# Attention scores of two layers: contraction groups of 32 rows with two masked key copies in four half-filled PSUM banks, in place of groups of 64 rows with four copies in two full banks

## The chip, the cores and the metric

The kernel runs on one core of one Trainium2 chip. The metric is the device time of one execution in microseconds (us), as the median of several executions. Lower is better. All arithmetic is fp32.

## The reference, cut to what matters

32 sequences of 64 tokens and 256 features go through four layers. Layer 0 is a small cross attention, layers 1 and 2 are transformer blocks (self attention, cross attention with a context, MLP), and layer 3 is a recurrent block. The change is in layers 1 and 2:

```python
NH = 16; HD = 16                      # 16 heads of 16 features
def attention(q, k, v, mask):
    scores = jnp.einsum('bhqd,bhkd->bhqk', q, k) / jnp.sqrt(jnp.float32(HD))
    scores = scores * mask - 10000.0 * (1.0 - mask)
    probs = jax.nn.softmax(scores, axis=-1)
    return jnp.einsum('bhqk,bhkd->bhqd', probs, v)
...
qkv = layernorm(hidden_states, ln1_s, ln1_b) @ w_qkv + b_qkv
q, k, v = jnp.split(qkv, 3, axis=-1)
ctx = merge_heads(attention(split_heads(q), split_heads(k), split_heads(v), ltor_mask))
x = hidden_states + ctx @ w_ao + b_ao
q = layernorm(x, ln2_s, ln2_b) @ w_q + b_q
k, v = jnp.split(encoder_states @ w_kv + b_kv, 2, axis=-1)
ctx = merge_heads(attention(split_heads(q), split_heads(k), split_heads(v), cross_mask))
x = x + ctx @ w_co + b_co
return x + gelu(layernorm(x, ln3_s, ln3_b) @ w1 + b1) @ w2 + b2
```

## The kernel before

`phase_a` is layer 0, `phase_b` is layers 1 and 2, and `phase_c` is layer 3. In `phase_b` the 2048 tokens are four groups of 512 tokens, and two layers make eight **turns** (`TURNS`), each for one group in one layer. A turn has eight **steps** k: 0 to 3 are self attention and 4 to 7 cross attention, each for 128 tokens (two sequences of 64). Turns 1 to 6 are one hardware loop. All engines follow an order written out by hand in their function `turn`, and they meet only through semaphores.

Heads have 16 features and a matmul operand starts at row 0, 32, 64 or 96, so heads are not multiplied one by one. The keys are written several times, each copy with all heads but one of every group of rows set to zero (`keys` on ACT, which multiplies by the 0/1 column `lane[:, m]` and adds a bias that is zero elsewhere; `NM` copies). One matmul then gives the scores of `NM` heads of one group of rows. Before the change a group is 64 rows (`HALF`), with `NM` = 4.

PSUM has eight banks of 512 fp32 columns. `SC, PT, CX, CO, YB = 0, 2, 4, 5, 6`: the scores (`SC`) take banks 0 and 1, the transposed probabilities (`PT`) banks 2 and 3, and the projections and the MLP banks 6 and 7.

One step of attention passes over four engines:

- `scores(n, k)` on PE: before the change eight matmuls of 64 rows, 64 stationary and 256 moving columns. Each fp32 matmul is two passes, and each pass is one record in the trace. They wait until DVE has read the scores of tile k-1 (`mul_ok`).
- `mask(n, k)` on DVE (L1346): reads the scores out of PSUM, multiplies by the mask and raises `mul_ok`. `add_mask` on POOL (L786) adds the other half of the mask.
- `maximum` (L1353) and `subtract` (L1358) on DVE, `exps` on ACT (L1204).
- `probs_T(n, k)` on PE (L983): eight transposes into banks 2 and 3, after `exp_ok`. `copy_pT` on ACT (L1209) copies them out.
- `times_v` on PE (L998) waits for that copy; then DVE `normalize` (L1364, L1366), PE `result_T` (L1006) and ACT `copy_cT` (L1214).

PE issues `scores(k+2)` right behind `times_v(k)`, so the scores of tile k+1 are written before `probs_T(k)` and those of tile k+2 after it. Steps 3 and 4 of `turn` on PE read:

```python
times_v(n, 3)
next_scores(n, 3, nxt)      # scores of tile 5
hidden(prev, 5, nxt)        # L1036, MLP of the turn before
probs_T(n, 4)
result_T(n, 3)
norm_T_mid(n, 2)            # L899
norm_T_in(nxt, prev)        # L893
queries_mid(n, 2)           # L956
```

DVE does in step 3: `maximum` of tile 4, `pre` 3, `subtract` of tile 4, `residual` 2, `pre` 4, `normalize` 3, `norm` 2, `pre` 5 (L1404), and then `mask` of tile 5. The self-attention keys of the first group are made at the end of `phase_a`, chunk 0 on ACT (L472) and chunk 1 on DVE (L553).

Of the kernel before, what the change touches and what calls it, by code (L numbers as in the profile page):

```python
# [17 lines left out]
ALU = mybir.AluOpType  # L18
# [3 lines left out]
P = 128  # L22
B, S, D = 32, 64, 256
# [5 lines left out]
NC = D // P  # L29
NH, HD = 16, 16  # L30
NPAIR = NH // 2
HALF = P // 2
NM = HALF // HD
VW = HD + 1
DFF = 1024
NJ = DFF // P
# [12 lines left out]
def packed(**sets):  # L49

    cols, spans, at = {}, {}, 0
    for s, parts in sets.items():
        start = at
        for n, width in parts:
# [8 lines left out]
                              out=(("co", D),), hidden=(("w1", DFF),))  # L63
VL, VL_SETS, VL_COLS = packed(first=(("ln1_s", 2), ("ln1_b", 2), ("bq", 2), ("bk", NC * NM)),
                              middle=(("ln2_s", 2), ("ln2_b", 2), ("bq2", 2), ("bk2", NC * NM)),
                              hidden=(("ln3_s", 2), ("ln3_b", 2), ("b1", NJ)))
# [507 lines left out]
def phase_b(nc, io, ps, w, x_mid, ld_b, ld_c, ld_set, zero_ok, a_stored, b_loads, entry, stored, c_loads, head):  # L574

    ctx = ExitStack()
    with ctx:
# [3 lines left out]
        def sem(name):  # L581
            return ctx.enter_context(nc.semaphore("b_" + name))
# [13 lines left out]
        qT, kB, vP = ([w[a + n] for a in ("self", "cross")] for n in ("_q", "_k", "_v"))  # L596
        sc = w["sc"]
# [19 lines left out]
        sc_ps, mul_ok, add_ok, max_ok, sub_ok, exp_ok = (sem(n) for n in ("sc_ps", "mul_ok", "add_ok", "max_ok", "sub_ok", "exp_ok"))  # L617
# [8 lines left out]
        TILES = 2 * NP  # L626
# [11 lines left out]
        def tile(n, k):  # L638

            return TILES * n + k  # L640
# [6 lines left out]
        SC, PT, CX, CO, YB = 0, 2, 4, 5, 6  # L647
# [212 lines left out]
        def _(pe):  # L860
# [99 lines left out]
            def scores(n, k):  # L960
                a, p = k // NP, k % NP
                if a == 1:
                    pe.wait_ge(q_ok[1], tile(n, 2 * p) + 2)
                if p == 0:
                    pe.wait_ge(k_ok[a], 2 * n + 2)
                    if a == 0:
                        pe.wait_ge(q_ok[0], 2 * n + 2)
                after(pe, mul_ok, tile(n, k))
                pe.sem_inc(sc_go, 1)
                for c in range(NC):  # L970
                    for half in range(2):
                        f = slice(half * HALF, (half + 1) * HALF)
                        for b in range(2):
                            t = (2 * p + b) * S
                            mm = pe.matmul(ps[b * S:(b + 1) * S, SC + half, c * D:(c + 1) * D], qT[a][f, c, t:t + S],
                                           kB[a][f, c, 2 * p + b, :, :].rearrange("f m k -> f (m k)"), start=True, stop=True)
                mm.then_inc(sc_ps, 1)

            def probs_T(n, k):
                pe.wait_ge(exp_ok, tile(n, k) + 1)  # L980
                for half in range(2):
                    for i in range(NPAIR // 2):
                        mm = pe.transpose(ps[:, PT + half, i * P:(i + 1) * P],  # L983
                                          sc[:, k % 2, half, 2 * i:2 * i + 2, :].rearrange("q i k -> q (i k)"), w["ident"][:, :])
                    mm.then_inc(pT_ps, 1)
# [79 lines left out]

            def turn(n, prev, nxt):

                probs_T(n, 0)
                last_project(n, 0, prev)
                keys_ctx(n, 0, prev)  # L1070
                times_v(n, 0)
                next_scores(n, 0, nxt)
                keys_ctx(n, 1, prev)
                result_T(n, 0)
                values_ctx(n, 0)

                probs_T(n, 1)
                last_project(n, 1, prev)
                values_ctx(n, 1)
                times_v(n, 1)  # L1080
                next_scores(n, 1, nxt)
                norm_T_mlp(prev, n)
                result_T(n, 1)
                norm_T_mid(n, 0)
                hidden(prev, 0, nxt)
                queries_mid(n, 0)

                probs_T(n, 2)
                last_project(n, 2, prev)
                hidden(prev, 1, nxt)  # L1090
                times_v(n, 2)
                next_scores(n, 2, nxt)
                hidden(prev, 2, nxt)
                hidden(prev, 3, nxt)
                result_T(n, 2)
                norm_T_mid(n, 1)

                probs_T(n, 3)
                queries_mid(n, 1)
                hidden(prev, 4, nxt)  # L1100
                last_project(n, 3, prev)
                times_v(n, 3)
                next_scores(n, 3, nxt)
                hidden(prev, 5, nxt)
                probs_T(n, 4)
                result_T(n, 3)
                norm_T_mid(n, 2)
                norm_T_in(nxt, prev)

                queries_mid(n, 2)  # L1110
                queries_in(nxt, 0)
                last_project(n, 4, prev)
                times_v(n, 4)
                next_scores(n, 4, nxt)
                queries_in(nxt, 1)
                result_T(n, 4)
                norm_T_mid(n, 3)
                keys_in(nxt, 0)
                queries_mid(n, 3)

                probs_T(n, 5)
                last_project(n, 5, prev)
                keys_in(nxt, 1)
                times_v(n, 5)
                next_scores(n, 5, nxt)
                hidden(prev, 6, nxt)
                result_T(n, 5)
                hidden(prev, 7, nxt)

                probs_T(n, 6)  # L1130
                last_project(n, 6, prev)
                values_in(nxt, 0, prev)
                times_v(n, 6)
                next_scores(n, 6, nxt)
                mlp_out(prev, 0, nxt)
                result_T(n, 6)
                mlp_out(prev, 1, nxt)

                probs_T(n, 7)
                last_project(n, 7, prev)  # L1140
                values_in(nxt, 1, prev)
                times_v(n, 7)
                next_scores(n, 7, nxt)
                mlp_out(prev, 2, nxt)
                result_T(n, 7)
                mlp_out(prev, 3, nxt)
# [8 lines left out]
            n = TURNS - 1  # L1155
# [134 lines left out]
        def _(dve):  # L1290
# [49 lines left out]
            def mask(n, k):  # L1340
                a, p = k // NP, k % NP
                if a == 1 and p == 0:
                    dve.wait_ge(cmask_ok, 2 * n + 2)
                dve.wait_ge(sc_ps, tile(n, k) + 1)
                m = (self_mul[:, :], cross_mul[:, p, :])[a]
                dve.tensor_tensor(sc[:, p % 2, :, :, :].rearrange("q f i k -> q (f i) k"),  # L1346
                                  ps[:, SC:SC + 2, :].rearrange("q f (i k) -> q (f i) k", k=S),
                                  m.unsqueeze(1).broadcast_to([P, NH, S]), ALU.mult).then_inc(mul_ok, 1)

            def maximum(n, k):  # L1350
                dve.wait_ge(add_ok, tile(n, k) + 1)
# [171 lines left out]
            n = TURNS - 1  # L1523
# [1276 lines left out]
```

## Time and profile before

| | |
|---|---|
| median of 3 runs | 1195.87 us (1191.57 to 1198.06) |
| span of the profiled execution | 1193.7 us |
| busy share of the span | PE 90%, PE weight loads 60%, DVE 70%, ACT 46%, POOL 36% |
| records of matmul passes | 8032 |
| matmul passes of the scores (L975) | 1024, 71.8 us busy |
| key copies on ACT (L1197) | 120 activations, 83.8 us |
| length of a turn in the loop, from one `probs_T(n, 0)` to the next | 89.4 us |

The span goes from the first to the last instruction of one profiled execution; the page gives no other time of that execution, and the runs without the profiler are a separate measurement. The busy digits of an engine are tenths of one fortieth of the span. PEclk is the clock that was granted to TensorE, in tenths of full speed. In a timeline row the first number is the start, the second the length of the merged piece, and the bracket gives how long the engine sat idle before it and what released it. A piece of several matmuls holds as many passes as its x count says.

### The profile page before, as it was taken

To read this page: it belongs to the slowest core of one execution; us is meant where nothing else is said; L and a number is where in the kernel's file an instruction comes from. 1 tells how busy PE (TensorE), PEld (TensorE's weight loads), DVE (VectorE), ACT (ScalarE), POOL (GpSimd) and SP (SyncE) were. 2 spreads that over 40 slices of the span, in tenths; PEclk is the share of its full clock that TensorE was granted. 3 is DMA by queue.
4 is the path that set the end of the run, shared out by engine and by line. 5 is a ranking of instruction groups with operands and counts; after the bars stand their busy time and mean duration, and the time that the engine had idled before them with its cause. 6 is when DMAs were issued, how large, how long until landed. Compare 5 with 4: busy or idle time off the path is not lost. (4 is left out here: it accounts for less than half of the span.)

```text
span 1193.7 us, 21696 instructions
## 1 busy us (share of the span) xinstructions
PE 1070.6 (90%) x8032; PEld 714.9 (60%) x8032; DVE 832.5 (70%) x1575; ACT 546.1 (46%) x1016; POOL 433.2 (36%) x387
## 2 busy tenths in 40 slices
PE   7987797999999999999999999978986888979866
PEld 6875565668668668668668668656363353443524
DVE  3665776876876876876876876873448687796864
ACT  4653453474474474474474474462231434414331
POOL 2111443442442442442442442331317427264250
PEclk9998978999999999999999999999997999989998
DMA  7130100001002002102101001030010010010100
GB/s 251 62 98 18 42 1 19 24 2 36 22 0 71 22 0 79 35 0 67 60 0 35 22 1 35 1 122 18 1 36 21 1 36 20 0 35 3 36 1 18
DMA packets 37952, 40.28 MB, mean 34 GB/s; under 512 B 8640, under 2 KB 33536, under 8 KB 37648
## 3 DMA queue, kind: packets, MB, share of 16 engines
q1 hardware_dynamic: 37776, 39.55, 10.3%
q8 instruction: 29, 0.48, 0.2%
q14 instruction: 19, 0.16, 0.0%
q0 software_dynamic: 128, 0.10, 0.0%
HBM read 31.26 MB, written 8.39 MB: 33 GB/s over the span
## 5 line engine op out<-in xcount | busy, mean ns | idle before, releaser
L1353 DVE TENSOR_REDUCE b_neg_max<-head_area 128x16 f32<-128x1024 f32 x64 | 77.8, 1216 | 89.2 <-POOL head_area L786 88.7
L791 POOL TENSOR_TENSOR b_rstd<-b_var,minus_half 128x1 f32<-128x1 f32 x63 | 34.5, 548 | 250.0 <-DVE b_var L1382 250.0
L2101 POOL TENSOR_TENSOR c_rs<-c_st,head_area 128x512 f32<-128x512 f32 x64 | 88.7, 1415 | 97.3 <-DVE c_st L2580 95.7
L1204 ACT ACTIVATE head_area<-head_area 128x1024 f32<-128x1024 f32 x64 | 68.0, 1062 | 112.1 <-DVE head_area L1358 111.6
L1036 PE MATMUL ps<-b_hT_mlp,wl 128*128 128x512 f32 x224 | 108.9, 608 | 7.5 <-DVE b_act_g L1404 6.3
L1050 PE MATMUL ps<-w,b_act_g 128*128 128x256 f32 x448 | 102.8, 383 | 2.7 <-ACT b_act_g L1222 2.7
L786 POOL TENSOR_TENSOR head_area<-head_area,b_self_add 128x1024 f32<-128x1024 f32 x32 | 75.4, 2355 | 79.5 <-DVE head_area L1346 79.5
L786 POOL TENSOR_TENSOR head_area<-head_area 128x1024 f32<-128x1024 f32 x32 | 75.3, 2354 | 77.1 <-DVE head_area L1346 77.1
L1209 ACT ACTIVATE head_area<-ps 128x512 f32<-128x512 f32 x128 | 70.1, 607 | 63.0 <-PE ps L983 62.9
L1050 PEld LDWEIGHTS ps<-w,b_act_g 128*128 128x128 f32 x448 | 82.9, 190 | 17.6 <-issue 4.6
L869 PE MATMUL ps<-head_area,wl 128*128 128x512 f32 x176 | 85.9, 611 | 0.0
L1358 DVE TENSOR_TENSOR head_area<-head_area,b_neg_max 128x1024 f32<-128x1024 f32 x64 | 78.1, 1220 | 1.2
L2580 DVE TENSOR_TENSOR_SCAN c_st<-head_area,ps 128x512 f32<-128x512 f32 x64 | 73.7, 1203 | 3.8 <-ACT ps L2388 3.8
L983 PE MATMUL ps<-ident,head_area 128*128 128x128 f32 x512 | 70.1, 282 | 4.2 <-ACT head_area L1204 4.2
L1019 PE MATMUL ps<-wl,b_cT 128*128 128x256 f32 x252 | 68.3, 395 | 2.9 <-ACT b_cT L1214 1.4
L983 PEld LDWEIGHTS ps<-ident,head_area 128*128 128x128 f32 x512 | 61.2, 146 | 15.4 <-issue 8.1
L1036 PEld LDWEIGHTS ps<-b_hT_mlp,wl 128*128 128x128 f32 x224 | 38.6, 190 | 49.9 <-issue 30.5
L879 PE MATMUL ps<-wl,head_area 128*64 128x128 f32 x1024 | 64.5, 280 | 0.2 <-ACT head_area L1197 0.2
L879 PEld LDWEIGHTS ps<-wl,head_area 128*64 128x64 f32 x1024 | 57.0, 140 | 9.7 <-issue 7.2
L1214 ACT ACTIVATE b_cT<-ps 128x256 f32<-128x256 f32 x64 | 24.6, 384 | 77.2 <-PE ps L1006 77.2
L1019 PEld LDWEIGHTS ps<-wl,b_cT 128*128 128x128 f32 x252 | 45.0, 194 | 15.2 <-issue 6.9
L1396 DVE TENSOR_TENSOR b_x_out<-ps,b_x_mlp 128x256 f32<-128x256 f32 x28 | 11.9, 425 | 57.0 <-PE ps L1050 48.6
(262 smaller groups left out, 2321.1 us busy)
## 6 DMA issues: line engine op xcount, KB each, us to landing
head_area<-x_mid SPq DMA_DIRECT2D x9, 512.0 KB, 3.8
wl<-in_wl SPq DMA_DIRECT2D x4, 1024.0 KB, 6.9
head_area<-in_ctxT SPq DMA_DIRECT2D x8, 512.0 KB, 3.6
x_mid<-b_x_out SPq DMA_DIRECT2D x8, 512.0 KB, 2.9
area<-in_wc SPq DMA_DIRECT2D x1, 2336.0 KB, 8.1
a_x_in<-in_x SPq DMA_DIRECT2D x16, 128.0 KB, 3.0
a_y_in<-in_ctx SPq DMA_DIRECT2D x16, 128.0 KB, 3.7
w<-in_w SPq DMA_DIRECT2D x2, 1024.0 KB, 9.5
```

Of the source, the lines that this page charges most:

```text
L786: pool.tensor_tensor(t, t, m.unsqueeze(1).broadcast_to([P, NH, S]), ALU.add).then_inc(add_ok, 1)
L869: mm = pe.matmul(ps[:, YB + c, :], weight(name, k, first + c * P, first + (c + 1) * P), rhs[:, k, :], start=(k == 0), stop=(k == NC - 1))
L879: mm = pe.matmul(ps[odd * S:(odd + 1) * S, YB + half, b * P:(b + 1) * P], lhs[:, k, t:t + S], weight(name, k, odd * P, (odd + 1) * P), sta ...
L983: mm = pe.transpose(ps[:, PT + half, i * P:(i + 1) * P], sc[:, k % 2, half, 2 * i:2 * i + 2, :].rearrange("q i k -> q (i k)"), w["ident"][ ...
L1019: mm = pe.matmul(ps[:, CO, OUT], cT[:, half, p * P:(p + 1) * P], weight(("ao", "co")[a], half), start=(half == 0), stop=(half == 1))
L1036: mm = pe.matmul(ps[:, YB + j % 2, :], weight("w1", k, j * P, (j + 1) * P), hT_mlp[:, k, :], start=(k == 0), stop=(k == NC - 1))
L1050: mm = pe.matmul(ps[:, YB + MLP_BANK[p], 0:D], act_g[:, j, p * P:(p + 1) * P], w["w2"][:, j, :], start=(j == 0), stop=(j == NJ - 1))
L1209: act.activation(pT[:, b, :, :].rearrange("k i q -> k (i q)"), ps[:, PT + b, :], ACT.Copy).then_inc(pT_ok, 1)
L1353: dve.tensor_reduce(neg_max[:, k % 2, :], t, AX, ALU.max, negate=True).then_inc(max_ok, 1)
L1358: dve.tensor_tensor(t, t, neg_max[:, k % 2, :].unsqueeze(2).broadcast_to([P, 2 * NPAIR, S]), ALU.add).then_inc(sub_ok, 1)
L2101: pool.tensor_tensor(rs[:, i % BUFS, :], st[:, i % 3, :], rF[:, i // RS, :], ALU.mult).then_inc(rs_ok, 1)
L2580: dve.tensor_tensor_scan(st[:, i % 3, :], decay[:, i // RS, :, :].rearrange("f b t -> f (b t)"), ps[:, VB[i % 4], :], 0.0, ALU.mult, ALU.a ...
```

## The change

Groups of rows become 32 rows (`ROWS`), so there are four of them (`NR`), with two masked copies (`NM` = 2). A score matmul has 32 rows, 64 stationary and 128 moving columns, and there are 16 per tile. Group r writes columns 0 to 255 of bank r, so the scores lie in banks 0 to 3, of which 2 and 3 are also `PT`. `mask` reads four half banks. `probs_T(n, k)` gets one more wait, for `mask` of tile k+1, which still lies in banks 2 and 3. The order of all steps is the same on every engine. The host lays the heads out in another order, so that the probabilities keep their shape.

```diff
-HALF = P // 2
-NM = HALF // HD
+ROWS = P // 4
+NR = P // ROWS
+NM = ROWS // HD
...
                 for c in range(NC):
-                    for half in range(2):
-                        f = slice(half * HALF, (half + 1) * HALF)
+                    for r in range(NR):
+                        f = slice(r * ROWS, (r + 1) * ROWS)
                         for b in range(2):
                             t = (2 * p + b) * S
-                            mm = pe.matmul(ps[b * S:(b + 1) * S, SC + half, c * D:(c + 1) * D], qT[a][f, c, t:t + S],
+                            mm = pe.matmul(ps[b * S:(b + 1) * S, SC + r, c * P:(c + 1) * P], qT[a][f, c, t:t + S],
                                            kB[a][f, c, 2 * p + b, :, :].rearrange("f m k -> f (m k)"), start=True, stop=True)
                 mm.then_inc(sc_ps, 1)
 
-            def probs_T(n, k):
+            def probs_T(n, k, nxt):
+                if k + 1 < TILES or nxt is not None:
+                    pe.wait_ge(mul_ok, tile(n, k) + 2)
                 pe.wait_ge(exp_ok, tile(n, k) + 1)
...
-                dve.tensor_tensor(sc[:, p % 2, :, :, :].rearrange("q f i k -> q (f i) k"),
-                                  ps[:, SC:SC + 2, :].rearrange("q f (i k) -> q (f i) k", k=S),
-                                  m.unsqueeze(1).broadcast_to([P, NH, S]), ALU.mult).then_inc(mul_ok, 1)
+                dve.tensor_tensor(sc[:, p % 2, :, :, :].rearrange("q h (f i) k -> q (h f) i k", f=2),
+                                  ps[:, SC:SC + NR, 0:D].rearrange("q r (i k) -> q r i k", k=S),
+                                  m.unsqueeze(1).unsqueeze(1).broadcast_to([P, NR, NH // NR, S]), ALU.mult).then_inc(mul_ok, 1)
...
-    lane = np.arange(P) % HALF // HD
+    lane = np.arange(P) % ROWS // HD
...
-        v = m.reshape(m.shape[:-1] + (NC, 2, NM // 2, 2, HD))
+        v = m.reshape(m.shape[:-1] + (NC, NR, NM, HD))
```

The eight calls of `probs_T` pass `nxt` as well. `keys` on ACT and the two places of `phase_a` that write keys loop over `NM`, so they lose half of their instructions without an edit of their own.

## Rows read from the trace of the kernel before

**Rows 1.** The page's slices of the span: PE, PE weight loads, DVE and granted clock
```profile
PE   7987797999999999999999999978986888979866
PEld 6875565668668668668668668656363353443524
DVE  3665776876876876876876876873448687796864
PEclk9998978999999999999999999999997999989998
```

**Rows 2.** Busy time (x instructions), granted clock, DMA share, GB/s of one turn of the loop
```profile
382.08:471.49 89.41, 87.33 (x801) 61.80 (x800) 65.85 (x127) 48.13 (x76) 32.62 (x29) 1.00 0.10 34
```

**Rows 3.** Timeline of PE in step 0 of that turn: times_v, scores of tile 2, next operation
```profile
385.63 1.13 PE L998 MATMUL ps<-area,head_area 128*64 128x34 f32 x32
386.69 1.09 PE L975 MATMUL ps<-area 64*64 64x256 f32 x16
387.71 1.99 PE L869 MATMUL ps<-head_area,wl 128*128 128x512 f32 x4
```

**Rows 4.** The same PE records, windows 386.69:386.80, 387.10:387.30 and 387.50:387.80
```profile
386.69 0.45 PE L975 MATMUL ps<-area 64*64 64x256 f32 x4
...
386.95 0.83 PE L975 MATMUL ps<-area 64*64 64x256 f32 x12
...
387.17 0.61 PE L975 MATMUL ps<-area 64*64 64x256 f32 x8
```

**Rows 5.** Timeline of PE, window 842.26:842.30: matmuls of 32 rows in the next phase
```profile
842.26 0.70 PE L1667 MATMUL ps<-head_area,area 32*128 32x512 f32 x2
```

**Rows 6.** Timeline of PE in steps 2 to 4 of the same turn
```profile
402.04 1.04 PE L983 MATMUL ps<-ident,head_area 128*128 128x128 f32 x8
...
410.69 1.98 PE L1036 MATMUL ps<-b_hT_mlp,wl 128*128 128x512 f32 x4 [0.93 <-DVE b_act_g L1404]
...
412.95 1.04 PE L983 MATMUL ps<-ident,head_area 128*128 128x128 f32 x8
...
419.76 1.99 PE L1036 MATMUL ps<-b_hT_mlp,wl 128*128 128x512 f32 x4
421.58 1.04 PE L983 MATMUL ps<-ident,head_area 128*128 128x128 f32 x8
...
422.92 0.44 PE L899 MATMUL ps<-ident,b_xc 128*128 128x128 f32 x2
...
425.08 1.16 PE L956 MATMUL ps<-head_area,wl 128*128 128x128 f32 x8 [0.84 <-ACT head_area L1177]
...
443.89 1.99 PE L1036 MATMUL ps<-b_hT_mlp,wl 128*128 128x512 f32 x4 [0.19 <-ACT area L1197]
```

**Rows 7.** Timeline of DVE in the same turn, from normalize of tile 0 to mask of tile 5
```profile
386.81 0.26 DVE L1364 RECIPROCAL b_inv_sum<-ps 128x16 f32<-128x16 f32 x1 [0.34 <-PE ps L998]
...
387.85 1.23 DVE L1346 TENSOR_TENSOR head_area<-ps,b_self_mul 128x1024 f32<-128x1024 f32 x1
...
399.01 1.22 DVE L1346 TENSOR_TENSOR head_area<-ps,b_self_mul 128x1024 f32<-128x1024 f32 x1
...
405.72 1.22 DVE L1353 TENSOR_REDUCE b_neg_max<-head_area 128x16 f32<-128x1024 f32 x1 [3.44 <-POOL head_area L786]
...
411.49 1.22 DVE L1346 TENSOR_TENSOR head_area<-ps,head_area 128x1024 f32<-128x1024 f32 x1
...
423.44 1.21 DVE L1346 TENSOR_TENSOR head_area<-ps,head_area 128x1024 f32<-128x1024 f32 x1
```

**Rows 8.** Timeline of ACT around step 4 of the same turn
```profile
420.05 1.06 ACT L1204 ACTIVATE head_area<-head_area 128x1024 f32<-128x1024 f32 x1 [3.25 <-DVE head_area L1358]
...
424.24 0.79 ACT L1177 ACTIVATE head_area<-ps,vl 128x128 f32<-128x128 f32 x2
```

**Rows 9.** Timeline of PE in turns 0 and 7 and behind them: idle stretches and what follows
```profile
190.21 0.44 PE L1006 MATMUL ps<-ident,head_area 128*128 128x128 f32 x2 [3.01 <-DVE head_area L1366]
190.49 1.04 PE L983 MATMUL ps<-ident,head_area 128*128 128x128 f32 x8
...
200.62 0.69 PE L1006 MATMUL ps<-ident,head_area 128*128 128x128 f32 x2 [4.40 <-DVE head_area L1366]
201.10 1.92 PE L983 MATMUL ps<-ident,head_area 128*128 128x128 f32 x8
...
827.57 0.44 PE L1627 MATMUL ps<-ident,b_xc 128*128 128x128 f32 x2 [1.41 <-DVE b_xc L1836]
830.24 5.48 PE L1654 MATMUL ps<-head_area,area 128*128 128x512 f32 x8 [2.24 <-DVE head_area L1858]
```

**Rows 10.** PE busy (x), granted clock, DMA share, GB/s of a stretch after 4.40 us idle
```profile
200.70:205.60 4.90, 4.90 (x16) 0.50 0.00 0
```

**Rows 11.** Timeline at the seam of phase_a and phase_b
```profile
104.41 2.96 DVE L553 TENSOR_SCALAR area<-ps,lane,vl 128x512 f32<-128x512 f32 x4
...
105.83 0.72 POOL L330 TENSOR_TENSOR a_x_out<-a_x_keep,a_gate 128x256 f32<-128x256 f32 x1 [4.14 <-ACT a_gate L454]
...
107.95 1.99 PE L975 MATMUL ps<-area 64*64 64x256 f32 x16 [2.71 <-PEq L203]
```

More of the change, by code:

```diff
@@ L1066, in turn @@
             def turn(n, prev, nxt):
-                probs_T(n, 0)
+                probs_T(n, 0, nxt)
                 last_project(n, 0, prev)
@@ L1075, in turn @@
                 values_ctx(n, 0)
-                probs_T(n, 1)
+                probs_T(n, 1, nxt)
                 last_project(n, 1, prev)
@@ L1086, in turn @@
                 queries_mid(n, 0)
-                probs_T(n, 2)
+                probs_T(n, 2, nxt)
                 last_project(n, 2, prev)
@@ L1096, in turn @@
                 norm_T_mid(n, 1)
-                probs_T(n, 3)
+                probs_T(n, 3, nxt)
                 queries_mid(n, 1)
@@ L1104, in turn @@
                 hidden(prev, 5, nxt)
-                probs_T(n, 4)
+                probs_T(n, 4, nxt)
                 result_T(n, 3)
@@ L1119, in turn @@
                 queries_mid(n, 3)
-                probs_T(n, 5)
+                probs_T(n, 5, nxt)
                 last_project(n, 5, prev)
@@ L1128, in turn @@
                 hidden(prev, 7, nxt)
-                probs_T(n, 6)
+                probs_T(n, 6, nxt)
                 last_project(n, 6, prev)
@@ L1137, in turn @@
                 mlp_out(prev, 1, nxt)
-                probs_T(n, 7)
+                probs_T(n, 7, nxt)
                 last_project(n, 7, prev)
@@ L2749, in by_value @@
     def by_value(m):
-        return heads_in(m, 3, 1, 0, 2, 4)
+        return heads_in(m, 2, 1, 0, 3)
     def by_context(m):
-        return heads_in(m, 1, 0, 2, 3, 4)
+        return heads_in(m, 1, 0, 2, 3)
     wl, w2, vl, rl = [], [], [], []
```

## The prediction, made before the changed kernel ran

> **What bounds the kernel now.** I read the page's slices first. From slice 8 to slice 26, the loop of turns in `phase_b`, PE stands at 9 in every slice at full clock, while DVE is at 6 to 8 [rows 1]. The table of one turn agrees: 87.33 of 89.41 us busy on PE, 65.85 on DVE, 48.13 on ACT [rows 2]. So a turn lasts as long as PE's work plus its few gaps, and I looked for these in PE's timeline: 0.93, 0.84 and 0.19 us [rows 6]. The first waits for DVE (`pre`), the other two for ACT. The page's share of 90% is an average with the other phases and says nothing on the change.
>
> The second thing to read is DVE's timeline, because the change ties PE to DVE at a new place. From `normalize` of tile 0, which a PE operation releases at 386.81, to the end of `mask` of tile 5 at 423.44 + 1.21 = 424.65, DVE has one idle stretch, the 3.44 us before 405.72, and that one ends with POOL's `add_mask`, which itself follows DVE's statistics [rows 7]. Within these 37.8 us nothing that PE does faster makes DVE earlier. The reader is to see that: DVE is not the bound of the turn, but of this stretch.
>
> **The scores themselves.** Today they take 387.71 - 386.69 = 1.02 us of PE's time per tile, for 16 passes [rows 3]. The 16 passes start in four rounds of four: four within the first 0.11 us, and rounds at 386.69, 386.95, 387.17, so 0.26 for the first interval and 0.22 for the next [rows 4]. A round is four places of the array (two row groups by two halves of the columns) that run at the same time; 0.216 us fits 256 columns. After the change there are eight places, still four rounds, and a round has 128 columns, so about 0.109 us. The trace has matmuls of 32 rows at two places starting within 0.04 us of each other [rows 5], so groups of 32 rows do run beside each other. Four rounds by (0.216 - 0.109) is 0.43 us saved per tile, and 0.6 us are left. The bounds: all of the 1.02 may scale with columns (0.51 saved), or each pass may have a floor of its own. The nearest row for that is `times_v`, whose 32 passes of only 34 columns take 386.69 - 385.63 = 1.06 us, 33 ns each [rows 3]. If that is a floor, 32 score passes cost 1.06 again and nothing is saved. I take 0.43, since that row has only two places and weight loads of 128 rows between its passes.
>
> Four passes start within the first 0.11 us, under 30 ns each [rows 4]. The Trainium skill (TensorEngine Tiling (Array Packing), Instruction Overhead) gives each matmul about 60 cycles of overhead on trn2 and advises not to take the tiling factor from a dimension that is already small. By it, an estimate, 32 passes of 25 ns (60 cycles at 2.4 GHz) would be 0.80 us, 0.22 saved and not 0.43. It is the rule that speaks against the change; no run here shows it for 128 columns.
>
> **Where the saving counts.** The loop has eight sets of scores per turn. Those of steps 1 to 3 lie ahead of the new wait, inside the stretch that DVE now sets, and that of step 0 ends as `mask` of tile 2 starts anyway (387.85, after `norm`) [rows 7]: these four are lost in the wait. Those of steps 4 to 7 lie on PE's dense path from step 4 to the next turn: 4 x 0.43 = 1.7 us per turn gained (bounds 0 and 2.0).
>
> **The new wait.** `probs_T(k)` must now wait for `mask` of tile k+1. In step 2 the transposes start at 402.04, `mask` has ended at 400.23: room. In step 3 it is 412.95 against 412.71: just in time [rows 6, 7]. In steps 0, 1, 5, 6 and 7 the `mask` ended over 2 us earlier. In step 4 it is not: the transposes start at 421.58 [rows 6], `mask` of tile 5 ends at 424.65 [rows 7]. Only `hidden(prev, 5)` stands between the scores of tile 5 and `probs_T` of tile 4, while DVE has five more instructions ahead of that `mask`. With some 0.15 us for the semaphore and the first weight load, the transposes start at 424.8, 3.2 us late. Queued behind them on PE are `result_T`, `norm_T_mid`, `norm_T_in` and `queries_mid`. The last of these had waited 0.84 us for ACT, whose L1177 was held up by a gelu until 424.24 [rows 6, 8]. Now L1177 waits for `norm_T_mid`: PE reaches its end 422.92 + 0.44 - 421.58 = 1.78 after the transposes' start, at 426.6; L1177 takes 0.79 (the row, for its two pieces); `queries_mid` starts at 427.5 in place of 425.08. So of 3.2 us, 0.8 is taken out of an old gap, and **2.4 us per turn** are lost (bounds 2.2 and 2.6).
>
> **Two small gains.** Key copies: 60 activations of some 0.7 us leave ACT. Only the gap of 0.19 us before `hidden` in step 5 hangs on them [rows 6]; elsewhere ACT has room (48 of 89 us, [rows 2]), so 0.2 us per turn. If ACT were the bound they would be worth 5 us per turn. At the seam, DVE's four key copies (2.96 us from 104.41) end the phase; two fewer end at 105.9, and then POOL's last addition, at 106.55, is the last: 0.8 us. The first scores there take 1.99 us [rows 11], and I give them 0.7: together 1.5 us, once. `mask` reads the same 1024 elements in four runs: no change (bounds 0 and 0.1 us).
>
> **The clock.** The new stall leaves PE idle from about 421.1 (its scores of tile 5 and `hidden` come 0.4 earlier) to 424.8, over 3 us, in every turn. The trace has an idle stretch of 3.01 us after which eight transposes take the usual 1.04 us, and one of 4.40 us after which they take 1.92 [rows 9], with a granted clock of 0.50, which is 1.2 GHz, over at least 4.9 us [rows 10]. Idles of 1.41 and 2.24 us with 0.44 of work between them were also followed by slow matmuls: eight passes of 512 columns in 5.48 us [rows 9]. The new idle lies between these, so I expect the low clock after some of the stalls but not all: two in three. A low stretch of 3.4 to 6.8 us on PE's dense path costs half of its length, 1.7 to 3.4; I take 2.3. Two thirds of it is 1.5 us per turn (bounds 0 and 2.9).
>
> **The sum.** Turns 1 to 6: 6 x (2.4 - 1.7 - 0.2 + 1.5) = +12.0. Turn 0 waits on DVE and POOL with idle PE, so neither part counts: 0. Turn 7 has PE idle as well; +0.5. The seam: -1.5. In all +11 us against the profiled span of 1193.7; the runs' median is 2.2 above that span, and I move it by the same: 1195.87 + 11 = **1207 us**.
>
> **Rivals.**
>
> *The stall without the clock* (0.25). Speaking for it: the 3.01 us row. Then 6 x (2.4 - 1.9) + 0.5 - 1.5 = +2: 1198, no measurable difference.
>
> *A floor per pass* (0.2). The scores stay at about 1.02 us. Then 6 x (2.4 - 0.2 + 1.5) + 0.5 - 0.8 = +22: 1218. For it: 33 ns per pass in `times_v`. Against it: rounds in which four passes start within 0.11 us. The page's 60 cycles lie between this and the forecast: by its 0.80 us, an estimate, the sum would be +16, 1212; I give that 0.07 of these 0.2.
>
> *The wait costs nothing* (0.08), on the other side. It would need `mask` of tile 5 before the end of `exps` of tile 4 at 421.11 [rows 8], which PE waits for already; that is 3.5 us sooner. It could come so if the DVE stretch began earlier, through ACT's lighter load or earlier scores. Below a stall of about 1.2 us the kernel is faster by more than 0.5%; with none, 6 x (-1.9) - 1.5 = -13: 1183. Against it: DVE's stretch has no gap that ends with PE or ACT.
>
> *The forecast* has 0.47, from 1202 to 1213.
>
> **The numbers.** About 0.5% (6 us) is what a measurement of this kernel can tell from no change. Faster comes from the last rival, 0.07. Same takes the stall without the clock and the low end of the forecast: 0.27. Slower is the rest: 0.66. The range of 8 in 10 takes in the stall without the clock and most of the floor: 1194 to 1220.
>
> **What the changed profile would show.** The step of the wait: PE idle over 3 us before L983 in step 4, released by DVE L1346, in turns 1 to 7, and nowhere else by that line over 0.3. The scores: x32 passes in about 0.6 us from start to next start. The clock: 0.50 in the stretch behind some of these stalls. ACT: half of the key copies and no gap before `hidden` in step 5. The turn: 91.4 us on average in place of 89.4. The prediction is wrong if the scores do not shrink, if the low clock is absent or comes each time, or if DVE reaches `mask` of tile 5 at another time after `normalize` of tile 0 than 37.8 us.

## The result, and the profile after

The changed kernel takes **1211.38 us** (median of 4 runs, 1208.84 to 1220.81) against 1196.96 us for the kernel before on the same chip: a ratio of 1.014 with a 95% interval of 1.0115 to 1.0167 (the two medians by themselves give 1.012; the four runs spread widely). So it is slower by 14 us, as forecast in sign, and 4 us above the 1207 that I gave. The profiled execution has a span of 1209.2 us, 15.5 above that of before.

The page's slices of the changed kernel (PE, weight loads, DVE, granted clock):

```profile
PE   7988687989989989989989989987995888978866
PEld 5866565668658668658668668656363353443524
DVE  4645766766766766766766766764449687796864
PEclk9979988999999999999999989998998999999998
```

Against [rows 1], PE has lost its unbroken nines: every third slice of the loop is an 8. The table of four turns of the loop (turns 1 to 4; columns as in [rows 2]) shows what a count of busy time misses:

```profile
204.22:296.99 92.77, 86.93 (x929) 64.09 (x929) 63.45 (x127) 43.30 (x68) 35.74 (x31) 0.96 0.05 14
296.99:388.90 91.91, 85.43 (x928) 62.77 (x929) 64.19 (x129) 43.45 (x68) 32.76 (x29) 0.98 0.10 32
388.90:480.15 91.25, 85.43 (x929) 62.79 (x929) 63.10 (x127) 43.56 (x68) 32.75 (x29) 0.98 0.10 35
480.15:569.97 89.82, 84.08 (x929) 61.20 (x929) 63.54 (x128) 43.20 (x68) 32.75 (x29) 1.00 0.08 25
```

PE is busy for 84 to 87 us of a turn where it was 87.33 [rows 2], and yet the turn is longer. Note the last row: one turn of 89.82 us at a clock of 1.00, and the others longer at 0.98 or less. PE's timeline of step 0 and of steps 3 and 4 of the turn from 388.90 shows both sides of the change:

```profile
392.51 1.13 PE L1001 MATMUL ps<-area,head_area 128*64 128x34 f32 x32
393.56 0.69 PE L976 MATMUL ps<-area 32*64 32x128 f32 x32
394.19 1.98 PE L870 MATMUL ps<-head_area,wl 128*128 128x512 f32 x4
...
425.67 0.69 PE L976 MATMUL ps<-head_area 32*64 32x128 f32 x32
426.30 1.98 PE L1039 MATMUL ps<-b_hT_mlp,wl 128*128 128x512 f32 x4
431.64 1.10 PE L986 MATMUL ps<-ident,head_area 128*128 128x128 f32 x8 [3.36 <-DVE head_area L1349]
432.57 0.55 PE L1009 MATMUL ps<-ident,head_area 128*128 128x128 f32 x2
432.91 0.64 PE L900 MATMUL ps<-ident,b_xc 128*128 128x128 f32 x2
433.34 1.92 PE L894 MATMUL ps<-ident,xc_in 128*128 128x128 f32 x8
435.05 1.55 PE L957 MATMUL ps<-head_area,wl 128*128 128x128 f32 x8
```

The scores take 394.19 - 393.56 = 0.63 us where [rows 3] have 1.02. The transposes of tile 4 follow 3.36 us of idle that DVE's `mask` (L1349) ends. Behind them eight transposes take 1.92 us, which is the length they have at half the clock; the same stretch as a window (columns as in [rows 2]):

```profile
431.64:436.43 4.79, 4.79 (x28) 4.79 (x29) 2.34 (x2) 2.48 (x5) 3.73 (x3) 0.64 0.00 0
```

DVE's timeline of the same turn, from `normalize` of tile 0 to `mask` of tile 5, to be set beside [rows 7]:

```profile
393.68 0.26 DVE L1367 RECIPROCAL b_inv_sum<-ps 128x16 f32<-128x16 f32 x1 [1.39 <-PE ps L1001]
...
426.87 0.41 DVE L1378 TENSOR_TENSOR b_x_cur<-ps,head_area 128x256 f32<-128x256 f32 x1
...
428.10 0.75 DVE L1407 TENSOR_SCALAR b_act_g<-ps,vl 128x512 f32<-128x512 f32 x1
...
429.39 0.40 DVE L1390 TENSOR_SCALAR b_xc<-b_x_cur,b_mv,b_rstd 128x256 f32<-128x256 f32 x1
429.71 0.74 DVE L1407 TENSOR_SCALAR b_act_g<-ps,vl 128x512 f32<-128x512 f32 x1
430.38 1.21 DVE L1349 TENSOR_TENSOR head_area<-ps,head_area 128x1024 f32<-128x1024 f32 x1
```

From 393.68 to 431.59 it is 37.9 us, as before. PE's faster scores make none of it earlier.

### The profile page after: what moved, and what is told of

Read it like the earlier page. It is cut to its first block and busy times, and to the rows that moved or that the text cites. A ratio compares the mean times of both kernels' runs of the same rounds, so it can differ in the third digit from the quotient of the medians.

```text
span 1209.2 us, 23743 instructions
## 1 busy us (share of the span) xinstructions
PE 1057.0 (87%) x9056; PEld 722.7 (60%) x9056; DVE 816.1 (67%) x1573; ACT 509.4 (42%) x954; POOL 434.1 (36%) x387
## 3 DMA queue, kind: packets, MB, share of 16 engines
q8 instruction: 82, 1.34, 0.5%
## 5 line engine op out<-in xcount | busy, mean ns | idle before, releaser
L1356 DVE TENSOR_REDUCE b_neg_max<-head_area 128x16 f32<-128x1024 f32 x64 | 77.9, 1218 | 113.9 <-POOL head_area L787 113.5
L1053 PE MATMUL ps<-w,b_act_g 128*128 128x256 f32 x448 | 105.5, 390 | 2.9 <-ACT b_act_g L1225 2.9
L986 PE MATMUL ps<-ident,head_area 128*128 128x128 f32 x512 | 75.2, 295 | 35.0 <-DVE head_area L1349 33.4
L1180 ACT ACTIVATE head_area<-ps,vl 128x128 f32<-128x128 f32 x64 | 25.7, 453 | 53.2 <-PE ps L900 52.7
```

What stands on the lines that cost most here:

```text
L986: mm = pe.transpose(ps[:, PT + half, i * P:(i + 1) * P], sc[:, k % 2, half, 2 * i:2 * i + 2, :].rearrange("q i k -> q (i k)"), w["ident"][ ...
L1053: mm = pe.matmul(ps[:, YB + MLP_BANK[p], 0:D], act_g[:, j, p * P:(p + 1) * P], w["w2"][:, j, :], start=(j == 0), stop=(j == NJ - 1))
L1356: dve.tensor_reduce(neg_max[:, k % 2, :], t, AX, ALU.max, negate=True).then_inc(max_ok, 1)
```

## The experiments

Eleven kernels ran, each beside the kernel before on the same chip; the ratios below are to that kernel, with their 95% intervals. Three questions: is it the wait that costs, what does the clock add to it, and what would take the wait away?

**1. The wait alone.** The kernel before, with the two lines of the wait and nothing else:

```diff
-            def probs_T(n, k):
+            def probs_T(n, k, nxt):
+                if k + 1 < TILES or nxt is not None:
+                    pe.wait_ge(mul_ok, tile(n, k) + 2)
                 pe.wait_ge(exp_ok, tile(n, k) + 1)
```

> The kernel before with nothing changed but the new wait: TensorE doesn't begin a tile's transposes before the mask of the next tile has run. Scores, banks and key copies stay as they were (16 passes of 256 columns, four masked copies). Theory (the wait is what costs): about 2.4 us more of waiting ahead of the transposes of tile 4 in each turn, the granted clock falls to about half behind it in most turns and costs some 1.2 more, and no gain of the cheaper scores stands against it; seven turns of 3.2 to 3.6 give plus 22, about 1218 us. Rival (the wait is free, and the changed kernel loses by its short matmuls or its banks): within 3 us of before, about 1197.

Measured: 1222.95 us, ratio 1.022 (1.0199 to 1.0234), 5 us above the 1218 of the theory. The profile is of the slowest of the five runs (1232.69 us); it has 4.8 us in turn 0 (85.40 for 80.63) and 2.8 us of idle at the heads of turns 2 to 6 that the theory didn't have. PE's timeline of step 4 in two turns of this kernel:

```profile
441.73 1.10 PE L985 MATMUL ps<-ident,head_area 128*128 128x128 f32 x8 [2.96 <-DVE head_area L1348]
...
443.09 1.04 PE L893 MATMUL ps<-ident,xc_in 128*128 128x128 f32 x8
```

```profile
533.69 1.97 PE L985 MATMUL ps<-ident,head_area 128*128 128x128 f32 x8 [2.96 <-DVE head_area L1348]
...
536.30 1.92 PE L893 MATMUL ps<-ident,xc_in 128*128 128x128 f32 x8
```

The wait is the same to 10 ns in both, and the clock falls in one and not in the other. The turns that these and the like rows belong to, as windows:

```profile
399.06:491.04 91.98, 87.47 (x801) 61.76 (x801) 64.91 (x127) 48.23 (x76) 32.59 (x29) 1.00 0.10 34
491.04:585.60 94.56, 90.03 (x801) 64.56 (x801) 66.04 (x128) 48.51 (x76) 32.57 (x29) 0.96 0.08 24
...
678.96:770.45 91.49, 87.29 (x801) 61.88 (x802) 65.66 (x127) 48.33 (x76) 32.59 (x29) 1.00 0.06 20
```

The two at a clock of 1.00 lasted 91.98 and 91.49 us. That is 2.3 and 2.1 more than the 89.4 of before, once 0.30 us of idle at the end of the first is taken off. The second is the cleaner one, since no such idle ends it (experiment 5 shows that a turn with it is longer by a little more than the idle): 2.1 us is the stall by itself. The rest of the change then gives back 1222.95 - 1211.38 = 11.6 us by the medians, the other side of the sum.

**2. The clock.** The changed kernel with PE kept at work in the wait, by matmuls whose result nothing reads:

```diff
+            def fill(n):
+                pe.wait_ge(res_ok, tile(n, 2) + 1)
+                for _ in range(3):
+                    pe.matmul(ps[:, CO, :], w["ident"][:, :], w["ident"][:, :].unsqueeze(1).broadcast_to([P, 4, P]), start=True, stop=True)
...
                 hidden(prev, 5, nxt)
+                fill(n)
                 probs_T(n, 4, nxt)
```

> The changed kernel plus three matmuls of 128 x 512 whose result nothing reads (identity by identity into a bank that is free), issued ahead of the transposes of tile 4, where TensorE otherwise stands still; they take up the 3.4 us stretch of waiting and don't shorten it. Theory (part of the loss is the lower clock behind the stall): the low granted clock behind the transposes of tile 4 is gone in the loop's turns, the transposes of norm(2) take about 1.0 us in place of 1.9, and the time falls by 1.2 us a turn, about 1203. If the three matmuls last beyond the mask's end, that part goes off again. Rival (the lower clock is a companion and not a cost, since VectorE sets the pace there anyway): same as the changed kernel, 1211.

Measured: 1202.12 us, ratio 1.003 (1.0014 to 1.0046), 9 us under the changed kernel for three more matmuls a turn.

```profile
425.14 2.74 PE L1072 MATMUL ps<-ident 128*128 128x512 f32 x6
428.65 1.09 PE L986 MATMUL ps<-ident,head_area 128*128 128x128 f32 x8 [0.78 <-DVE head_area L1355]
...
430.02 1.04 PE L894 MATMUL ps<-ident,xc_in 128*128 128x128 f32 x8
```

PE still begins its transposes when DVE lets it. From scores to transposes nothing is faster, 428.65 - 422.70 = 5.95 us against 431.64 - 425.67 = 5.97 in the changed kernel. What differs is 1.04 for 1.92 us on what follows. The windows behind the wait, in the changed kernel (turns 3 and 4) and then in this one (turn 3), show it in the clock:

```profile
431.64:437.64 6.00, 6.00 (x31) 5.36 (x32) 2.44 (x2) 3.49 (x9) 3.73 (x3) 0.72 0.00 0
522.86:528.86 6.00, 5.97 (x36) 4.54 (x36) 2.45 (x2) 4.43 (x10) 3.73 (x3) 1.00 0.00 0
```

```profile
428.65:433.65 5.00, 4.97 (x32) 3.97 (x33) 2.44 (x2) 3.43 (x9) 3.73 (x3) 1.00 0.00 0
```

In turns 1 to 7 the changed kernel has the low clock in six of these seven windows, this kernel in none. Turns 1 to 6 are 8.5 us shorter here (539.97 for 548.47), and 7.6 of it stands in step 4, from one `probs_T` to the next: 12.69 or 12.70 us in each of the six turns, where the changed kernel has 12.69 once and 13.98 to 15.04 otherwise. So the clock is a cost of its own beside the wait, 9 of the 14 us by the medians.

**3. Where DVE's work stands.** First the `mask` moved far ahead, right behind `subtract` of tile 4, in the changed kernel and, as a control, in the kernel before:

```diff
                 next_subtract(n, 3, nxt)
+                next_mask(n, 3, nxt)
                 last_residual(n, 3, prev)
                 pre(prev, 4)
                 normalize(n, 3)
                 last_norm(n, 3, prev)
                 pre(prev, 5)
-                next_mask(n, 3, nxt)
```

> The changed kernel with one instruction moved: VectorE's mask of tile 5 runs right behind the subtraction of tile 4, ahead of residual(2), normalise(3), norm(2) and the MLP steps that it used to follow. Theory (the loss is the wait of the transposes of tile 4 for that mask): the 3.4 us wait is gone, with it the low clock, and what stays is the cheaper scores; a turn comes out at about 88 to 89.5 us, the kernel at about 1190 us, faster than both. Rival (VectorE's work in that stretch is the bound, so that a mask ahead of it only moves the delay to residual(2) and normalise(3)): 1.2 us later in each turn than the gain, 1200 to 1205.

> The control to the run before: the same instruction moved in the kernel before, where no transposes wait for the mask. Theory: the order by itself gains nothing, as nothing waited for the mask of tile 5; it delays residual(2) and what follows it by up to 1.2 us a turn, so 1197 to 1205 us. Rival (the order is better by itself, whatever the wait): faster than before by more than 5 us, under 1191.

Measured: 1214.11 us (ratio 1.013, 1.0111 to 1.0151) and 1224.66 us (1.023, 1.0214 to 1.0243). The first is my rival's mechanism and costs more than its 1200 to 1205; the second is above both expectations. (The first one's profile is of an execution of 1208.38 us, near the fastest of six; four of them took 1213.5 to 1215.5.) PE and DVE in step 4 of the changed kernel with the `mask` early:

```profile
428.60 1.06 PE L986 MATMUL ps<-ident,head_area 128*128 128x128 f32 x8
431.08 0.44 PE L1009 MATMUL ps<-ident,head_area 128*128 128x128 f32 x2 [1.41 <-DVE head_area L1369]
432.86 0.67 PE L900 MATMUL ps<-ident,b_xc 128*128 128x128 f32 x2 [1.34 <-DVE b_xc L1390]
433.33 1.91 PE L894 MATMUL ps<-ident,xc_in 128*128 128x128 f32 x8
```

```profile
427.29 1.21 DVE L1349 TENSOR_TENSOR head_area<-ps,head_area 128x1024 f32<-128x1024 f32 x1
...
430.94 1.86 DVE L1390 TENSOR_SCALAR b_xc<-b_x_cur,b_mv,b_rstd 128x256 f32<-128x256 f32 x1
```

The wait for the `mask` is gone and two new ones stand behind it, for `normalize` and for `norm`, which the `mask` has made late. And `norm` takes 1.86 us where it takes 0.40, because POOL's `add_mask` now runs at the same time (last section). The low clock is there too, in step 4 of turns 1, 3, 5 and 7. In the kernel before, the same move costs 2.9 us a turn (92.3 for 89.4), with the low clock in step 4 of turns 2 to 7: it has no wait to gain from.

Then the two instructions that stand ahead of the `mask` and that nobody needs before it, `pre(4)` and `pre(5)`, put behind it, again in both kernels:

```diff
                 last_residual(n, 3, prev)
-                pre(prev, 4)
                 normalize(n, 3)
                 last_norm(n, 3, prev)
-                pre(prev, 5)
                 next_mask(n, 3, nxt)
+                pre(prev, 4)
+                pre(prev, 5)
```

> The changed kernel with VectorE's order around the wait altered in another place: the mask of tile 5 stays behind norm(2), but pre(4) and pre(5), 0.75 us each, now follow it instead of standing ahead of it. Theory (what sets TensorE's restart is VectorE's run of work up to norm(2) and then to the mask): the mask ends 1.3 to 1.5 us earlier, the wait ahead of the transposes of tile 4 falls from 3.36 to about 2.0 us, and with the lower clock still behind it the seven turns give back 7 x 1.35 = 9.5 us: about 1202 us; if the shorter stall leaves the clock full, 1195. Rival (norm(2) is held by GpSimd's reciprocal root, or the transposes of norm_in now wait for pre(5)): the gain goes to another wait, within 3 us of the changed kernel's 1211.

> The control to the run that moved pre(4) and pre(5) behind the mask of tile 5: the same two instructions moved in the kernel before, where no transposes wait for the mask. Theory (the order pays only because it shortens the new wait): TensorE's transposes of norm_in need pre(4) and pre(5), which now end 1.2 us later, behind a gap of 0.84 us that TensorE has there anyhow; so within 3 us of before, 1193 to 1199. Rival (the order is simply the better one): faster than before by 7 us or more, under 1189, and then the change of the scores would still cost what it cost.

Measured: 1194.05 us (ratio 0.999, 0.9978 to 1.0002) and 1196.70 us (1.000, 0.9983 to 1.0008). PE in step 4 of the changed kernel in this order:

```profile
424.04 1.09 PE L986 MATMUL ps<-ident,head_area 128*128 128x128 f32 x8 [2.14 <-DVE head_area L1349]
...
425.41 1.04 PE L894 MATMUL ps<-ident,xc_in 128*128 128x128 f32 x8
```

The wait fell by 1.22 us and the granted clock is 1.00 in the 5 us behind it in each of turns 1 to 7: some 17 us less for two instructions moved, 8.5 of them the wait (7 x 1.22), most of the rest the clock (step 4, counted from the start of its transposes, takes 12.69 or 12.70 us in turns 1 to 6, which is 7.6 us less in all than in the changed kernel). In the kernel before the same move is worth nothing. So the order was no fault in itself; the new wait made it one.

With two of the filling matmuls in what is left of the wait:

> The run before, plus two matmuls of 128 x 512 whose result nothing reads, in the remaining wait of about 2 us ahead of the transposes of tile 4. Theory: the two gains add, as the one is waiting and the other is the clock: 9.5 us of waiting and about 9 us of clock below the changed kernel, 1192 to 1196 us, level with or a little under the kernel before. Rival (the lower clock was already gone with the shorter stall): no faster than the run before it, and 0.0 to 0.5 us a turn slower where the two matmuls outlast the wait.

Measured: 1190.73 us, ratio 0.996 (0.9945 to 0.9974), a little faster than the kernel before. The time is 1.3 us below the 1192 to 1196 of my theory, and the mechanism is not the theory's: the clock was already full in the loop, as the rival had it, and turn 5 takes 88.58 us with and without the filling. The rival's time, no faster than the run before it, is missed as well, by 3 us. The profiles differ in turns 0 and 1, 80.62 and 90.07 us against 82.97 and 91.85, where PE waits most. In the 5 us behind the wait in step 4 of turn 0 the granted clock is 1.00 with the filling and 0.61 without; whether that is the filling or a difference between executions one profile each can't tell.

Last, half of `norm_in` (two of its four instructions; its second argument now says which two) put behind `pre(5)` as well, in both kernels:

```diff
                 pre(prev, 2)
-                norm_in(nxt if entry_of is None else entry_of)
+                norm_in(nxt if entry_of is None else entry_of, 0)
...
                 pre(prev, 4)
                 pre(prev, 5)
+                norm_in(nxt if entry_of is None else entry_of, 2)
```

> The run with pre(4) and pre(5) behind the mask, with one more shift in VectorE's order: of norm_in's four instructions of 0.95 us each (3.80 us ahead of the maximum of tile 4), the last two run behind pre(5), in VectorE's wait for GpSimd's addition. Theory (VectorE's run of work up to the mask of tile 5 is what TensorE waits for): the maximum of tile 4 begins 1.8 us earlier, as GpSimd's addition is done by then, the remaining wait of 2.14 us falls to about 0.3, and the seven turns give 7 x 1.8 = 12.6 us: about 1182, faster than both kernels. Rival (the transposes of norm_in, or the maximum of tile 5 behind it, now come late instead): within 4 us of the run it builds on, 1190 to 1198.

> The kernel before with both shifts of VectorE's order, for a fair comparison of the two forms of the scores. Theory (with the wait covered, what is left of the change is its cheaper scores, at 0.39 us a tile): this run is slower than the same order in the changed kernel by 5 to 15 us. Rival (before has no wait for the mask, so the shorter VectorE run gains it as much or more): it is as fast as the changed kernel in that order, or faster.

Measured: 1191.82 us (ratio 0.996, 0.994 to 0.9972) and 1210.52 us (1.012, 1.0099 to 1.0133). For the first the rival was right (1190 to 1198): the wait fell to 1.08 us, but the transposes of `norm_in` are late now, as PE's timeline shows:

```profile
514.89 1.09 PE L986 MATMUL ps<-ident,head_area 128*128 128x128 f32 x8 [1.08 <-DVE head_area L1349]
...
517.49 0.33 PE L894 MATMUL ps<-ident,xc_in 128*128 128x128 f32 x1 [0.85 <-DVE xc_in L1323]
518.22 0.77 PE L894 MATMUL ps<-ident,xc_in 128*128 128x128 f32 x5 [0.41 <-DVE xc_in L1323]
```

In the kernel before, whose transposes didn't wait for DVE there, that lateness is pure loss, with the low clock behind it (the eight passes of `queries_mid` take 1.92 us in place of 1.16). The two kernels in this order are 18.7 us apart, more than the 5 to 15 of the theory. The best orders found take the changed kernel from 1.4% slower than the kernel before to 0.4% faster.

**4. ScalarE's key copies back to four.** The changed kernel, with twice the room for key copies and twice as many of them, half of them read by nobody:

```diff
-                for m in range(NM):
+                for m in range(2 * NM):
                     op = act.activation(kB[a][:, c, :, m, :], ps[:, YB + c, :].rearrange("f (b k) -> f b k", k=S), ACT.Identity,
-                                        bias=vec(("bk", "bk2")[a], NM * c + m), scale=w["lane"][:, m:m + 1])
+                                        bias=vec(("bk", "bk2")[a], NM * c + m % NM), scale=w["lane"][:, m % NM:m % NM + 1])
```

> The changed kernel with ScalarE's key copies taken back to four activations a chunk in place of two (the two more write copies that nothing reads), all else as changed. It undoes the part of the change that I priced at 0.2 us a turn. Theory: the halved key copies hardly lie on the path, so this costs 0.2 to 0.5 us a turn, 1213 to 1215 us. Rival (the change lives on ScalarE's relief, and without it the loss would be much larger): 1 us a turn or more, over 1219.

Measured: 1213.67 us, ratio 1.016 (1.014 to 1.0186). That is 2.3 us above the changed kernel, 0.3 a turn, inside the theory's range; but the intervals overlap, and the traces say something else. Step 5 takes 9.96 or 9.97 us in each of turns 1 to 6 of this kernel and 9.11 in the changed one, and PE waits there for ACT's second chunk of keys:

```profile
456.09 1.98 PE L1039 MATMUL ps<-b_hT_mlp,wl 128*128 128x512 f32 x4 [0.59 <-ACT area L1200]
```

So in the loop the copies are worth 0.86 us a turn, which is nearer to the rival's 1 us than to the 0.2 to 0.5 of the theory. With four copies ACT holds PE up in that step whatever the scores cost: it takes 9.97 us in the kernel before, too. The profile of this kernel is 4.8 us longer in turns 1 to 6 (553.28 for 548.47) and over 4 us shorter from turn 7 on, where it has the full clock behind its wait and the changed kernel's profile hasn't. So these two executions are only 1.7 us apart, and the medians, of five and four runs, can't be trusted to 2 us either.

**5. Sixteen more instructions on PE's queue.** The kernel before, with each tile's wait for its exponentials written three times:

```diff
             def probs_T(n, k):
-                pe.wait_ge(exp_ok, tile(n, k) + 1)
+                for _ in range(3):
+                    pe.wait_ge(exp_ok, tile(n, k) + 1)
```

> The kernel before with 16 more instructions a turn on TensorE's queue that do nothing: each tile's wait for its exponentials is written three times. The run with only the new wait, 8 more instructions a turn, had 74 packets on the instruction queue where the kernel before has 29, and idle of 0.19 to 1.58 us with no releaser at the head of its loop turns. Theory (a loop body beyond some length is loaded again in each turn, and that costs by itself): 75 to 85 packets, idle at the head of the loop's turns of 0.2 to 1.6 us, 2 to 5 us in all, 1199 to 1202 us. Rival (the packets come for free, the gaps come from somewhere else): more packets, but within 1 us of before.

Measured: 1199.74 us, ratio 1.004 (1.0027 to 1.006). The pages of the kernel before, of this one and of the changed one, queue 8 (packets, MB, share):

```profile
q8 instruction: 29, 0.48, 0.2%
```

```profile
q8 instruction: 74, 1.21, 0.4%
```

```profile
q8 instruction: 82, 1.34, 0.5%
```

PE at the head of a turn in this kernel:

```profile
381.16 1.07 PE L984 MATMUL ps<-ident,head_area 128*128 128x128 f32 x8 [1.68 <-issue]
```

Idle of 1.68, 0.19, 0.23 and 0.30 us stands at the heads of turns 3 to 6, 2.4 us in all, and none there in the kernel before. The theory holds for time, packets (74, one short of its range) and place. The 16 bare waits by themselves cost next to nothing: turn 6, which no such idle ends, takes 89.43 us for the 89.40 of before. The turns that end with the idle are another 0.17 longer in their last step. Together it is 3.4 us in turns 1 to 6 (541.97 for 538.60), of the 4 us between the medians.

## Why the prediction was right, step by step

By PE's timelines the 15.5 us between the two spans are: 2.28 before the first transposes of `phase_b`, 0.84 in turn 0, 9.87 in turns 1 to 6 and 2.5 behind them.

The lengths of the steps, each from one `probs_T` to the next, at full clock (loading of instructions takes 0.32 us of the third row's last step, 0.16 of it the idle at its end):

| | 0 | 1 | 2 | 3 | 4 | 5 | 6 | 7 | turn |
|---|---|---|---|---|---|---|---|---|---|
| before, turn 3 | 9.66 | 10.30 | 10.91 | 8.63 | 14.17 | 9.96 | 12.89 | 12.89 | 89.41 |
| the wait alone, turn 6 | 9.71 | 10.28 | 10.91 | 11.74 | 13.09 | 9.97 | 12.89 | 12.89 | 91.49 |
| changed, turn 4 | 9.31 | 10.75 | 10.90 | 11.76 | 12.69 | 9.11 | 12.49 | 12.81 | 89.82 |

*The wait* (2.4 us a turn). Right in place and cause, a little large: step 4, `mask` of tile 5, 3.36 us of idle in turns 1 to 6 and 2.91 in turn 7. Alone (experiment 1) it made a turn 2.1 us longer. The transposes start 0.05 us behind the end of `mask` (431.59 and 431.64), for which I had 0.15, and at full clock `queries_mid` starts 2.43 us behind them (522.86 and 525.29), for which I had 2.7. The old gap of 0.84 us before `queries_mid` is gone, as the sum had it: 435.05 stands with no idle before it. "Nowhere else over 0.3" was wrong in turn 0, which has a wait for `mask` of 2.74 us in step 4 and four more of 0.44 to 4.65 us, and at the head of turn 1 (0.77 us). In step 1 a new wait of 0.83 us before `norm_T_mlp`, for DVE's `values`, is PE arriving sooner at DVE's stretch: there, as the prediction had it, the saving of the early steps is lost.

*The scores* (0.43 us a tile). 1.02 to 0.63, so 0.39 saved: four rounds of eight passes, as worked out (in the trace they start at 393.56, 393.72, 393.83 and 393.94), and 20 ns a pass (0.63 / 32). The floor per pass is not there at this size. The Trainium skill (TensorEngine Tiling (Array Packing), Instruction Overhead) would have 0.80 us, an estimate from its 60 cycles; the trace disagrees, with 20 ns a pass. Steps 4, 6 and 7 are 0.4 us shorter each than with the wait alone. Step 7 is read in turn 6, where it takes 12.49 us; with that, a turn at full clock lasts 89.50, which is 0.1 more than before, where the stall alone makes 2.1. So scores and key copies together give back 2.0 us; the sum had 1.9.

*The clock* (1.5 us a turn). Right in kind, a little large. The wait of 3.36 us was followed by the low clock in five of the six turns of the loop (I had four of six). Step 4 took 13.98, 14.01, 14.01, 12.69, 14.01 and 15.04 us in turns 1 to 6, so the cost was 1.3 us in four of them, 2.35 in one and none in one: 7.6 in all, where I had 9.0. Experiment 2 takes away just these 7.6.

*Key copies* (0.2 us a turn). Too small. The gap of 0.19 us is gone, but step 5 is 0.86 us shorter, of which the scores are 0.4: with four copies the wait for ACT would have grown to 0.59 us and eaten them (experiment 4). So the copies are worth 0.46 on top of the scores, and 0.86 if they alone are taken back.

*Turn 0, turn 7 and the seam.* In turn 0 I had nothing and there is 0.84; from turn 7 on I had 0.5 and there are 2.5, with the low clock behind the wait there (transposes of 1.97 us); the sum gave that no price. At the seam, the DVE copies take 1.52 us for 2.96 and the scores 0.97 for 1.99 [rows 11]:

```profile
108.30 1.52 DVE L554 TENSOR_SCALAR area<-ps,lane,vl 128x512 f32<-128x512 f32 x2
```

```profile
111.52 0.97 PE L976 MATMUL ps<-area 32*64 32x128 f32 x32 [2.38 <-PEq L204]
```

Yet the copies come 3.9 us later than before. That is no effect of the change that the runs can show: the first transposes of `phase_b` start at 118.62 to 124.61 us in the profiles of the six kernels that have the old code up to there (before's 120.47 among them), and at 118.83 to 124.90 in the seven with the new code. The 1.5 us of the seam lie inside that spread and were not resolved.

*What the sum lacked.* Instruction loading. At the heads of turns 2 to 5 PE has idle of 0.28, 0.94, 0.24 and 0.16 us that nothing in the trace releases, 1.62 in all, and none in the kernel before; the last steps of turns 1 to 5 are 0.7 longer besides. Experiment 5 shows such gaps with the old scores, banks and copies, for 4 us.

So turns 1 to 6 come to 6 x 0.1 for the stall less what is given back, 7.6 for the clock and 2.3 for loading, less 0.7 because the low stretch at the head of turn 1 costs 1.5 us and not the 2.2 of before: 9.8 of the measured 9.87. The prediction had 3.0 + 9.0 = 12.0: the stall and the clock too dear, no loading. These errors partly cancel, so the nearness of the loop's sum is in part luck; so is that its turns came out at 91.4 us on average, as forecast, since the kernel before has 89.8 by the same count, with its longer turn 1. That the runs show +14 against its +11 lies outside of these turns, where I had -1.0 and the two profiles show +5.6: 2.5 us from turn 7 on, 0.8 in turn 0, and 2.3 in a start of `phase_b` that varies. Of the rivals, the stall without the clock is one turn of this trace (89.82 us, 480.15 to 569.97), and experiment 2 made it the whole loop, at 1202 us where the rival had 1198; the floor per pass is excluded; the free wait would have needed another order of DVE's work, which experiment 3 supplied in part.

What stays open is why the same wait of 2.96 or 3.36 us is followed by the low clock in some turns and not in others; none of the runs varied it by itself. Nor is it settled how much of the 2.14 us of waiting that the moved `pre` instructions leave in each turn could still be had; one way was tried.

## What to carry to other kernels

A faster operation that shares its memory with another comes with a wait, and the wait's price is set by the order on the *other* engine: here two instructions of 0.75 us, harmless where they stood, were worth 17 us once the transposes waited behind them, and nothing without that wait. Before moving work away from in front of a late instruction, see that what is pushed back isn't the next thing waited for (with the `mask` far ahead nothing was gained). And count a stall of the matrix engine twice, once as time and once as clock.

## What the runs showed of the hardware that was not expected

**A loop may outgrow what TensorE keeps of its instructions.** The kernel before has 801 matmul passes and as many weight loads in a turn [rows 2] besides its waits, and from turn 2 to the end of turn 6 its queue 8 moves no packet. Eight more waits a turn (experiment 1) or 16 (experiment 5) brought 74 packets where 29 were, and the changed kernel has 82; each is 16 KB (1.34 MB / 82). In each of turns 2 to 5 it is 9 packets in the two experiments and 10 in the changed kernel, as its turn 4 shows (480.15 to 569.97):

```profile
q8 instruction: 10, 0.16, 0.7%
```

The Trainium skill (Advanced Engine Details and Errata, ISA Cache) gives 128 KB for TensorE, in lines of 16 KB or 256 instructions; the packets agree in size. Nine of 16 KB are 144 KB, an estimate, and more than the 128; and the changed kernel, whose turn has 256 records more (929 passes and loads for 801), has one more, so it looks as if the whole body of the loop were loaded anew in each turn. The visible price was idle of 0.16 to 1.68 us at the head of some turns.

**A GpSimd operation holds VectorE's up.** `norm` (128x256, source and result in SBUF, the on-chip memory) takes 0.40 us, and took 1.86 us in the changed kernel with the `mask` early, where POOL's addition of 2.35 us started 0.64 us before it:

```profile
430.30 2.35 POOL L787 TENSOR_TENSOR head_area<-head_area 128x1024 f32<-128x1024 f32 x1
```

VectorE's instruction ended about when POOL's did (432.80 and 432.65). `norm_in`'s four, of the same shape, took 3.81 us in the same way, and not 0.95 each, as I had counted. In the kernel before, from 413.29, they took 2.02 us beside POOL's addition (over at 415.15), 0.81 and 0.81 beside its two next ones, and 0.40 with POOL at rest. So the first two of them took 2.75 us in experiment 3's last pair where I had counted 1.9, and this is why the expected 0.3 us of waiting was 1.08. `pre`, which reads PSUM, took its usual length beside the same addition (0.75 us from 515.41, with POOL at work from 514.92 to 517.28). The Trainium skill (Trainium Architecture — The Big Picture, What this means for kernel authors) has the port that these two engines share as an exclusive lock; the rows agree.
